# A feed-forward loop over token tiles: the fourth tile's gate and up move right behind the third's

## The chip, the core and the metric

The kernel runs on one core of a Trainium2 chip. The metric is device time of one execution in microseconds (us). Before the change it is 1071.04 us, the median of 3 runs (1065.42 to 1078.87). Five engines work side by side, each through its own list of instructions in order, and meet through semaphores: TensorE (PE: matmuls and transposes; its weight loads are listed as PEld), VectorE (DVE), ScalarE (ACT), GpSimd (POOL) and SyncE (SP), which issues the DMAs here.

## What is computed

Four blocks over 16 sequences of 256 tokens with 128 features, each followed by a residual sum and a layer norm: a selective-scan block, a feed-forward block with quantised operands, a differential attention, and a three-layer perceptron with +1/-1 weights. The change touches the second one:

```
def fp4_quant_dequant(x):               # blocks of 16 along the last dimension
    scale = max(max|x| over the block / 6, 1e-12)
    xn = x / scale
    return nearest value of the grid {0, .5, 1, 1.5, 2, 3, 4, 6} to |xn|, * sign(xn) * scale

gate = quant(x) @ quant(w_gate).T        # 128 -> 352
y    = quant(x) @ quant(w_up).T          # 128 -> 352
h    = silu(gate) * y
out  = quant(h) @ quant(w_down).T        # 352 -> 128
x    = layernorm(x + out)
```

## The kernel before

The 4096 tokens are 32 tiles of 128, in 8 groups of 4 tiles. `x_all` keeps all tokens on chip. The phases follow each other: the scan, the feed-forward part, the attention, the perceptron, and neighbouring phases are interleaved at their borders.

The feed-forward part is a software pipeline written out by hand. Each engine has its own function `step(n)`, a generator of 8 pieces, and the order of the calls in it is the order of that engine's instructions. In step n:

- TensorE does gate and up of the four tiles of group n (`gate_up(n, j)`: the gate matmul is L1151, the up matmul L1153, each listed as two instructions), and for group n-2 the transposes of the quantised hidden tile (`turn`, L1164), the residual through an identity (`residual`, L1171) and the down projection (`down`, L1179). At its end it transposes group n+1's quantised x (L1108).
- ScalarE does the SiLU of each gate tile (`silu`, L1040), copies transposed tiles out of PSUM (`took_h`, L1047 and L1049), takes the absolute value of the hidden group n-1 (L1075) and of the x group n+2 (L1090), and squares and normalises group n-3 (L1056, L1063).
- VectorE multiplies SiLU and up (`hidden(n, j)`, L876), quantises the hidden group n (`scale_h`: maximum L914, scale L916, reciprocal L918, correction L920, scaling L923), takes the hidden group n-1 further (`magic_h` L928, `back_h` L934), and does the same for x of group n+2 (`scale_x` L885 to L894, `magic_x` L899, `back_x` L905). `magic` multiplies by a large number whose addition and subtraction rounds to the grid.
- GpSimd adds and subtracts it: for the hidden group n-1 L992 and L997, over 1408 columns, and for x of group n+2 L1004 and L1008, over 512 columns. It also takes the inverse root for the norm of group n-3 (L983, L986).

The order around the change in a step of VectorE is: `hidden 0`, `magic_h`, `hidden 1`, `scale_x`, `hidden 2`, `magic_x`, `hidden 3`, `scale_h`, `back_h`, `back_x`. GpSimd's list is: norm of n-3, L992, L997, L1004, L1008.

`hidden(n, j)` waits for the up matmul and the SiLU of its tile. `magic_x` waits for ScalarE's Abs (L1090), which waits for `scale_x`. L992 waits for `magic_h`, L997 for L992 by a semaphore, L1004 for `magic_x`. `scale_h` waits for all four tiles of the group. The gate matmul of tile j waits for the SiLU two tiles before (two banks of PSUM, `gp`); from step 6 (`LONE`) on there is one bank, because the attention has taken the other, and it waits for the SiLU of the tile before. The up matmul of tile j waits for the product two tiles before.

Steps -1 to 1 run beside the end of the scan, steps 2 to 5 alone, steps 6 to 10 beside the first pieces of the attention; that is written in `parts`, by `side_by_side`, which alternates the pieces of two generators. The attention's first pieces project and rotate a sequence: TensorE's L1644 over `a_xT`, ScalarE's copy L1606, GpSimd's multiplications L1502.

Of the kernel before, what the change touches and what calls it, by code (L numbers as in the profile page):

```python
# [63 lines left out]
def wait(eng, sem, value):  # L64

    if not (isinstance(value, int) and value <= 0):
        eng.wait_ge(sem, value)
# [119 lines left out]
def ffn_blocks(k, m):  # L187
    return k.x_all[:, bass.ds(GT * m, GT), :].rearrange("p a (b e) -> p (a b) e", e=QB)
# [555 lines left out]
def ffn_phase(nc, k, scan):  # L744
# [75 lines left out]
    def gate_bank(n, j):  # L820

        return gp[j % 2 if n < f.LONE else 0]

    def has(m):
        return 0 <= m < GROUPS
# [43 lines left out]
    def vector(dve):  # L869
        def hidden(n, j):  # L870
            if has(n):
                dve.wait_ge(up_ready, GT * n + j + 1)
                dve.wait_ge(silu_ready, GT * n + j + 1)
                if j == 0:
                    wait(dve, h_step, 5 * n)
                nc.vector.tensor_tensor(hid[:, j], sg[:, j], up[j % 2][:, 0:HID], ALU.mult).then_inc(hid_ready, 1)  # L876

        def scale_x(m):
            b = 5 * (m - 1)
            src = ffn_blocks(k, m)  # L880
            dve.wait_ge(x_back, m)
            dve.wait_ge(scan.norm_chain, m + 1)
            if m == 1:
                dve.wait_ge(scan.hcd_ready, scan.on_dve(GROUPS, 0))
            nc.vector.tensor_reduce(x_scale, src, AX.X, ALU.max, apply_absolute_value=True).then_inc(x_step, 1)  # L885
            dve.wait_ge(x_step, b + 1)
            nc.vector.tensor_scalar(x_scale, x_scale, 1.0 / 6.0, 1e-12, ALU.mult, ALU.max).then_inc(x_step, 1)
            dve.wait_ge(x_step, b + 2)
            nc.vector.reciprocal(x_inv, x_scale).then_inc(x_step, 1)
            dve.wait_ge(x_step, b + 3)  # L890
            nc.vector.tensor_scalar(x_inv, x_inv, 1.0 - 2.0 ** -22, None, ALU.mult).then_inc(x_step, 1)
            dve.wait_ge(x_step, b + 4)
            wait(dve, x_add, m - 1)
            nc.vector.tensor_tensor(qx.xs, src, x_inv.unsqueeze(2).broadcast_to([P, NXB, QB]),  # L894
                                    ALU.mult).then_inc(x_step, 1)

        def magic_x(m):
            dve.wait_ge(x_abs, m)
            nc.vector.tensor_scalar(qx.magic[:], qx.magic[:], 1.0, 2.0 ** 22 + 2.0, ALU.max,  # L899
                                    ALU.mult).then_inc(x_magic, 1)  # L900

        def back_x(m):
            dve.wait_ge(x_sub, m)
            dve.wait_ge(x_turned, m)
            nc.vector.tensor_tensor(qx.out, qx.q, x_scale.unsqueeze(2).broadcast_to([P, NXB, QB]),  # L905
                                    ALU.mult).then_inc(x_back, 1)

        def scale_h(m):
            b = 5 * m
            src = hid[:].rearrange("p a (b e) -> p (a b) e", e=QB)  # L910
            scale = h_scale[m % 2]
            dve.wait_ge(hid_ready, GT * m + GT)
            wait(dve, h_back, m - 1)
            nc.vector.tensor_reduce(scale, src, AX.X, ALU.max, apply_absolute_value=True).then_inc(h_step, 1)  # L914
            dve.wait_ge(h_step, b + 1)
            nc.vector.tensor_scalar(scale, scale, 1.0 / 6.0, 1e-12, ALU.mult, ALU.max).then_inc(h_step, 1)  # L916
            dve.wait_ge(h_step, b + 2)
            nc.vector.reciprocal(h_inv, scale).then_inc(h_step, 1)  # L918
            dve.wait_ge(h_step, b + 3)
            nc.vector.tensor_scalar(h_inv, h_inv, 1.0 - 2.0 ** -22, None, ALU.mult).then_inc(h_step, 1)  # L920
            dve.wait_ge(h_step, b + 4)
            wait(dve, h_add, m)
            nc.vector.tensor_tensor(hxs[:], src, h_inv.unsqueeze(2).broadcast_to([P, NHB, QB]),  # L923
                                    ALU.mult).then_inc(h_step, 1)

        def magic_h(m):
            dve.wait_ge(h_abs, m + 1)
            nc.vector.tensor_scalar(hmagic[:], hmagic[:], 1.0, 2.0 ** 22 + 2.0, ALU.max,  # L928
                                    ALU.mult).then_inc(h_magic, 1)

        def back_h(m):
            dve.wait_ge(h_sub, m + 1)
            wait(dve, h_turned, GT * (m - 1))
            nc.vector.tensor_tensor(hout[:, m % 2], hq[:], h_scale[m % 2].unsqueeze(2).broadcast_to([P, NHB, QB]),  # L934
                                    ALU.mult).then_inc(h_back, 1)

        nc.vector.memset(eps[:], LN_EPS).then_inc(const_ready, 1)

        def step(n):
            hidden(n, 0)  # L940
            yield
            if n == 0:
                back_x(1)
            if has(n - 1):
                magic_h(n - 1)
            yield
            hidden(n, 1)
            if has(n + 2):
                scale_x(n + 2)
            yield  # L950
            hidden(n, 2)
            if has(n + 2):
                magic_x(n + 2)
            yield
            hidden(n, 3)
            yield
            if has(n):
                scale_h(n)
            yield
            if has(n - 1):  # L960
                back_h(n - 1)
            yield
            if has(n + 2) and n >= 0:
                back_x(n + 2)
            yield

        return step
# [67 lines left out]
    def scalar(act):  # L1035
        def silu(n, j):
            if has(n):
                act.wait_ge(gate_ready, GT * n + j + 1)
                wait(act, hid_ready, GT * (n - 1) + j + 1)
                nc.scalar.activation(sg[:, j], gate_bank(n, j)[:, 0:HID], ACT.Silu).then_inc(silu_ready, 1)  # L1040

        def took_h(m, j):
            if has(m):
                act.wait_ge(h_turned, GT * m + j + 1)
                wait(act, down_ready, GT * m + j - 1)
                src = th[j % 2][:, 0:len(HC) * P].rearrange("p (c t) -> p c t", c=len(HC))
                nc.scalar.activation(hqT[:, j % 2, 0:full], src[:, 0:full], ACT.Copy)  # L1047
                rows = HC[-1][1]
                nc.scalar.activation(hqT[0:rows, j % 2, full], src[0:rows, full], ACT.Copy).then_inc(h_copied, 1)  # L1049

        def squares(m):

            act.wait_ge(down_ready, GT * m + GT)
            wait(act, rstd_ready, m)
            for j in range(GT):
                last = nc.scalar.activation(square[:, j], dn[:, j], ACT.Square, scale=DM ** -0.5,  # L1056
                                            accum_out=var[:, j:j + 1])
            last.then_inc(var_ready, 1)

        def normalize(m):  # L1060
            act.wait_ge(rstd_ready, m + 1)
            for j in range(GT):
                last = nc.scalar.activation(k.x_all[:, GT * m + j, :], dn[:, j], ACT.Copy, scale=rstd[:, j:j + 1])  # L1063
            last.then_inc(norm_chain, 1)

        def step(n):
            silu(n, 0)
            if has(n - 3):
                squares(n - 3)
            yield  # L1070
            m = n - 1
            if has(m):
                act.wait_ge(h_step, 5 * m + 5)
                wait(act, h_sub, m)
                nc.scalar.activation(hmagic[:], hxs[:], ACT.Abs).then_inc(h_abs, 1)  # L1075
            silu(n, 1)
            yield
            took_h(n - 2, 0)
            took_h(n - 2, 1)
            yield  # L1080
            if has(n - 3):
                normalize(n - 3)
            silu(n, 2)
            yield
            m = n + 2
            if has(m):

                act.wait_ge(x_step, 5 * (m - 1) + 5)
                wait(act, x_sub, m - 1)
                nc.scalar.activation(qx.magic[:], qx.xs, ACT.Abs).then_inc(x_abs, 1)  # L1090
            took_h(n - 2, 2)
            yield
            silu(n, 3)
            yield
            took_h(n - 2, 3)
            yield
            if has(n + 1) and n >= 0:
                took_x(act, n + 1)
            yield

        return step
# [37 lines left out]
    def tensor(pe):  # L1139
# [43 lines left out]
        def step(n):  # L1183
# [5 lines left out]
            turn(n - 2, 1)  # L1189
            yield  # L1190
            gate_up(n, 2)
            residual(n - 2)
            down(n - 2, 0)
            yield
            turn(n - 2, 2)
            down(n - 2, 1)
            yield
            gate_up(n, 3)
            yield
            turn(n - 2, 3)  # L1200
            down(n - 2, 2)
# [1084 lines left out]
```

## Time and profile before

| | |
|---|---|
| median of 3 runs | 1071.04 us |
| lowest, highest | 1065.42, 1078.87 us |
| the profiled execution | 1068.53 us, span 1066.7 us, mean granted TensorE clock 0.964 of full speed |
| busy over the span | PE 912.0 us (85%), DVE 891.7 (84%), POOL 788.1 (74%), ACT 731.5 (69%) |
| the feed-forward steps 0 to 5 | about 484 to 560 us of the span |

The feed-forward steps lie between the scan, which ends at about 477 us, and the attention, whose first maxima start at 596 us. Over the whole span DVE and PE are about equally busy, and the chain of waits (the chain of work that ended last, followed back from the last instruction) is shared between them: DVE 28%, PE 26%, issue 17%, ACT 15%, DMA 7%, POOL 4%. So one has to read the stage itself, from the timeline of each engine, which lists instructions in order of time with the idle time before each and what ended it.

### The profile page before, as it was taken

Reading aid. Unit: us, or ns where it says so; the run is one execution under the profiler, and the core shown is the slowest. Engines: PE = TensorE matmul, PEld = TensorE weight load, DVE = VectorE, ACT = ScalarE, POOL = GpSimd, SP = SyncE. Lnnn points to the kernel's source line nnn. Section 1 sums busy time; section 2 is a strip of 40 time slices with the busy share of each in tenths; the row PEclk is TensorE's granted clock in tenths of the full one; section 3 lists DMA queues with packets and bytes.
Section 4 is the critical chain, followed back from the end, with each engine's and each line's share of the span. In section 5 each row is a group of like instructions: output and inputs, shape, how many; then the busy total and the mean of one; then the engine's idle time right before and its main releaser. Section 6 shows DMA issues by size and latency. Waiting matters only on the chain.

```text
span 1066.7 us, 14636 instructions
## 1 busy us (share of the span) xinstructions
PE 912.0 (85%) x4466; PEld 481.7 (45%) x4482; DVE 891.7 (84%) x1337; ACT 731.5 (69%) x1600; POOL 788.1 (74%) x560
## 2 busy tenths in 40 slices
PE   7697979897989797786888679999999898699995
PEld 3233434342434343233556454565655543355453
DVE  4799999999999999998885667787777783479996
ACT  3776868686868686544565457777777768777872
POOL 2798998989898989875777734575756535767773
PEclk9899999899999999899999889999999999899998
DMA  4762535353434434003400323332323210000001
GB/s 149 318 239 79 205 113 200 118 199 119 177 142 152 166 141 177 0 1 81 66 0 16 104 76 90 92 99 83 99 83 102 80 47 2 0 2 12 18 21 30
DMA packets 35168, 104.03 MB, mean 98 GB/s; under 512 B 3659, under 2 KB 22475, under 8 KB 24395
## 3 DMA queue, kind: packets, MB, share of 16 engines
q1 hardware_dynamic: 35095, 103.16, 28.9%
q8 instruction: 34, 0.56, 0.2%
q14 instruction: 39, 0.32, 0.1%
HBM read 93.84 MB, written 8.91 MB: 96 GB/s over the span
## 4 chain that ended last, share of the span: by engine, by line
DVE 28%; PE 26%; issue 17%; ACT 15%; DMA 7%; POOL 4%; SPq 4%; DVEq 1%; POOLq 0%; ACTq 0%
PE bank L1644 11%; DVE bank L333 8%; PE bank L610 8%; DMA ks<-parts 6%; PE bank L2002 4%; DVE m_hC L342 4%; DVE a_nm L1410 3%; ACT bank L461 2%; DVE m_hS L333 2%; ACT L461 2%; SPq L1362 1%; DVE m_du L347 1%; SPq L1373 1%; DVE x_all L122 1%; DVE bank L914 1%
## 5 line engine op out<-in xcount | busy, mean ns | idle before, releaser
L610 PE MATMUL bank<-m_hC,ident 128*128 128x512 f32 x512 | 257.8, 627 | 61.4 <-POOL m_hC L568 22.7
L558 POOL TENSOR_TENSOR m_dBu<-m_du,m_Bt 128x1024 f32<-128x1024 f32 x128 | 299.3, 2356 | 12.6 <-DMA m_Bt<-bcd 11.8
L333 DVE TENSOR_TENSOR_SCAN bank<-bank,m_dBu 128x512 f32<-128x512 f32 x184 | 222.4, 1219 | 16.5 <-ACT bank L461 12.6
L1410 DVE TENSOR_REDUCE a_nm<-bank 128x2 f32<-128x512 f32 x256 | 169.3, 687 | 66.7 <-PE bank L1644 66.5
L1581 ACT ACTIVATE late<-bank 128x512 f32<-128x512 f32 x256 | 148.9, 600 | 65.2 <-PE bank L1644 63.4
L610 PEld LDWEIGHTS bank<-m_hC,ident 128*128 128x128 f32 x512 | 93.9, 196 | 203.9 <-issue 111.5
L461 ACT ACTIVATE bank<-m_delta,early 128x510 f32<-128x510 f32 x256 | 170.0, 677 | 0.3
L1644 PE MATMUL bank<-ks,qs 72*128 72x256 bf16 x512 | 100.4, 279 | 28.7 <-DMA ks<-parts 16.8
L342 DVE TENSOR_TENSOR m_hC<-bank,m_Ct 128x512 f32<-128x512 f32 x184 | 123.3, 670 | 0.0
L568 POOL TENSOR_TENSOR m_hC<-m_hS,m_Ct 128x512 f32<-128x512 f32 x72 | 94.6, 1315 | 26.6 <-DVE m_hS L333 26.6
L458 ACT ACTIVATE bank<-m_zero 128x2 f32<-128x2 f32 x181 | 31.2, 173 | 115.5 <-DVE m_hC L342 114.9
L1644 PE MATMUL bank<-qs,ks 99*128 99x256 bf16 x512 | 99.8, 277 | 4.5 <-ACT late L1581 3.1
L333 DVE TENSOR_TENSOR_SCAN m_hS<-bank,m_dBu 128x512 f32<-128x512 f32 x72 | 86.8, 1206 | 0.0
L2002 PE MATMUL bank<-qs,early 128*128 128x512 bf16 x374 | 85.7, 382 | 0.5
L1644 PEld LDWEIGHTS bank<-qs,ks 99*128 99x128 bf16 x512 | 43.3, 99 | 60.8 <-ACT late L1581 52.3
L1644 PEld LDWEIGHTS bank<-ks,qs 72*128 72x128 bf16 x512 | 44.6, 99 | 52.5 <-DVE a_nm L1410 25.3
L1644 PE MATMUL bank<-late,vx 128*32 128x512 f32 x512 | 68.0, 604 | 0.0
L1952 POOL TENSOR_TENSOR ks<-ks 128x512 f32<-128x512 f32 x32 | 38.5, 1204 | 32.7 <-ACT ks L1977 24.4
L610 PE MATMUL bank<-m_xT,m_wk 128*128 128x512 f32 x128 | 61.2, 624 | 0.0
L2002 PEld LDWEIGHTS bank<-qs,early 128*128 128x128 bf16 x384 | 37.3, 99 | 44.9 <-issue 2.8
L1518 POOL TENSOR_TENSOR a_part<-a_res,a_part 128x512 bf16<-128x512 f32 x16 | 18.5, 1155 | 47.4 <-ACT a_part L1600 47.4
L1525 POOL TENSOR_TENSOR a_rms<-a_ms_eps,neg_half 128x16 f32<-128x16 f32 x16 | 47.0, 2940 | 1.3
(217 smaller groups left out, 1797.1 us busy)
## 6 DMA issues: line engine op xcount, KB each, us to landing
m_Bt<-bcd SPq DMA_DIRECT2D x32, 1024.0 KB, 6.3
m_Ct<-bcd SPq DMA_DIRECT2D x32, 1024.0 KB, 6.6
qs<-parts SPq DMA_DIRECT2D x16, 576.0 KB
ks<-parts SPq DMA_DIRECT2D x48, 192.0 KB
parts<-a_part SPq DMA_DIRECT2D x32, 192.0 KB, 2.2
out<-x_all SPq DMA_DIRECT2D x8, 256.0 KB, 2.3
vx<-in_vrow SPq DMA_DIRECT2D x4, 256.0 KB
qs<-in_fill SPq DMA_DIRECT2D x1, 768.0 KB
```

Source lines behind the costliest of these rows:

```text
L333: nc.vector.tensor_tensor_scan(out, decay, dBu[:, g % RD], 0.0, ALU.mult, ALU.add).then_inc(scan_ready, 1)
L342: nc.vector.tensor_tensor(hC[:, g % RH], dA[g % RA][:].rearrange("p a b -> p (a b)"), Ct[:, s], ALU.mult).then_inc(hcd_ready, 1)
L461: nc.scalar.activation(dA[g % RA][:, :, 1:SEQ], delta[:, n % 2, c].rearrange("p (a b) -> p a b", a=2)[:, :, 1:SEQ], ACT.Exp, scale=decay[: ...
L558: nc.gpsimd.tensor_tensor(dBu[:, g % RD:g % RD + CH], du[:, n % 2], Bt[:, s].unsqueeze(1).broadcast_to([P, CH, GTOK]), ALU.mult).then_inc( ...
L568: nc.gpsimd.tensor_tensor(hC[:, g % RH], hS[:, on_pool(n, i) % RS], Ct[:, s], ALU.mult).then_inc(hcp_ready, 1)
L610: return nc.tensor.matmul(out, lhsT, rhs, start=start, stop=stop)
L1410: nc.vector.tensor_reduce(nm[:, slot % 2, q, 2 * pair:2 * pair + 2], s1[i % 2][:], AX.X, ALU.max, negate=True).then_inc(max_ready, 1)
L1525: nc.gpsimd.tensor_tensor(rms[:], ms_eps[:], k.neg_half[:, 0:TS * NH], ALU.pow).then_inc(rms_chain, 1)
L1581: nc.scalar.activation(pT[:, u // 2, u % 2], s2[u % 2][:], ACT.Exp, scale=float(HD) ** -0.25).then_inc(exp_ready, 1)
L1644: return nc.tensor.matmul(out, lhsT, rhs, start=start, stop=stop)
L1952: nc.gpsimd.tensor_tensor(rest_tile(s, c), full_tile(s, c), part_tile(s, q, c, 0), ALU.subtract).then_inc(s.rest_ready, 1)
L2002: return nc.tensor.matmul(out, lhsT, rhs, start=start, stop=stop)
```

## The change

In all three engines' `step(n)` the call for the fourth tile moves up to stand right behind the third tile's. On TensorE that is ahead of `residual`, `down 0`, `turn 2` and `down 1`; on ScalarE ahead of the Abs of x and `took_h 2`; on VectorE ahead of `magic_x`. Nothing is added or removed, and GpSimd's and SyncE's lists are the same.

```diff
@@ vector, step(n)
             hidden(n, 2)
+            hidden(n, 3)
             if has(n + 2):
                 magic_x(n + 2)
             yield
-            hidden(n, 3)
             yield
@@ scalar, step(n)
             silu(n, 2)
+            silu(n, 3)
             yield
             m = n + 2
             if has(m):
...
             took_h(n - 2, 2)
             yield
-            silu(n, 3)
             yield
@@ tensor, step(n)
             gate_up(n, 2)
+            gate_up(n, 3)
             residual(n - 2)
             down(n - 2, 0)
             yield
             turn(n - 2, 2)
             down(n - 2, 1)
             yield
-            gate_up(n, 3)
             yield
```

VectorE's list in a step from 2 to 5, around `magic_x`. L894 is the last instruction of `scale_x`, L876 the products of SiLU and up, L899 `magic_x`, L914 the first of `scale_h`.

```order
 L891 TENSOR_SCALAR bank<-bank 128x32
 L894 TENSOR_TENSOR early<-x_all,bank 128x512
-L876 TENSOR_TENSOR late<-late,bank 128x352
+L876 TENSOR_TENSOR late<-late,bank 128x352 x2
 L899 TENSOR_SCALAR early<-early 128x512
-L876 TENSOR_TENSOR late<-late,bank 128x352
 L914 TENSOR_REDUCE bank<-late 128x88
 L916 TENSOR_SCALAR bank<-bank 128x88
```

The product of the fourth tile now stands ahead of `magic_x` (L899), which stands directly before `scale_h`.

TensorE's list in the same steps, from the third tile's gate and up (L1151, L1153) on; L1171 is the residual, L1179 a down projection.

```order
 L1151 MATMUL bank<-early,late 128x352
 L1153 MATMUL bank<-early,late 128x352
+L1151 MATMUL bank<-early,late 128x352
+L1153 MATMUL bank<-early,late 128x352
 L1171 MATMUL bank<-x_all,ident 128x512
 L1179 MATMUL bank<-early,late 128x128 x3
```

The fourth tile's pair now stands ahead of the residual; before, it stood behind the second down projection.

## Rows read from the trace of the kernel before

**Rows 1.** Chain of waits, 470 to 690 us: start, duration, engine, tile and line.

```profile
526.71 0.53 DVE late L876
...
564.13 3.17 POOL late L992
```

**Rows 2.** Timeline, DVE, step 3: start, duration, engine, line, operation, shapes, [idle before].

```profile
520.52 0.51 DVE L876 TENSOR_TENSOR late<-late,bank 128x352 f32<-128x352 f32 x1
520.95 0.89 DVE L928 TENSOR_SCALAR late<-late 128x1408 f32<-128x1408 f32 x1
...
524.38 0.51 DVE L876 TENSOR_TENSOR late<-late,bank 128x352 f32<-128x352 f32 x1
525.16 0.43 DVE L899 TENSOR_SCALAR early<-early 128x512 f32<-128x512 f32 x1 [0.27 <-ACT early L1090]
526.71 0.52 DVE L876 TENSOR_TENSOR late<-late,bank 128x352 f32<-128x352 f32 x1 [1.12 <-PE bank L1153]
527.26 1.63 DVE L914 TENSOR_REDUCE bank<-late 128x88 f32<-128x1408 f32 x1
...
534.36 0.89 DVE L928 TENSOR_SCALAR late<-late 128x1408 f32<-128x1408 f32 x1
```

**Rows 3.** Timeline, DVE, steps 0 to 2: h2, then L928 and L914.

```profile
486.89 0.51 DVE L876 TENSOR_TENSOR late<-late,bank 128x352 f32<-128x352 f32 x1
...
488.65 1.63 DVE L914 TENSOR_REDUCE bank<-late 128x88 f32<-128x1408 f32 x1
...
494.71 0.90 DVE L928 TENSOR_SCALAR late<-late 128x1408 f32<-128x1408 f32 x1 [0.41 <-ACT late L1075]
...
499.90 1.63 DVE L914 TENSOR_REDUCE bank<-late 128x88 f32<-128x1408 f32 x1
...
507.00 0.89 DVE L928 TENSOR_SCALAR late<-late 128x1408 f32<-128x1408 f32 x1
...
513.86 1.63 DVE L914 TENSOR_REDUCE bank<-late 128x88 f32<-128x1408 f32 x1
```

**Rows 4.** Timeline, POOL, steps 3, 6 and 7.

```profile
521.92 3.17 POOL L992 TENSOR_TENSOR late<-late 128x1408 f32<-128x1408 f32 x1 [2.70 <-DVE late L928]
525.17 3.46 POOL L997 TENSOR_TENSOR late<-late 128x1408 f32<-128x1408 f32 x1
...
567.38 3.16 POOL L997 TENSOR_TENSOR late<-late 128x1408 f32<-128x1408 f32 x1
...
587.77 1.26 POOL L1502 TENSOR_TENSOR a_rc<-a_qk,aprm 128x512 f32<-128x512 f32 x1
```

**Rows 5.** Timeline, DVE, at two places outside the stage.

```profile
434.35 2.30 DVE L163 TENSOR_SCALAR early<-early 128x512 int32<-128x512 int32 x1
...
742.70 1.17 DVE L1428 CAST a_nmp<-a_nmr 128x32 bf16<-128x32 f32 x1
```

**Rows 6.** Timeline, POOL, at the same two places.

```profile
434.02 2.35 POOL L558 TENSOR_TENSOR m_dBu<-m_du,m_Bt 128x1024 f32<-128x1024 f32 x1
...
742.67 1.15 POOL L1518 TENSOR_TENSOR a_part<-a_res,a_part 128x512 bf16<-128x512 f32 x1 [2.65 <-ACT a_part L1600]
```

**Rows 7.** Timeline, PE, steps 2, 3 and 7.

```profile
506.10 1.54 PE L1164 MATMUL bank<-ident,late 128*128 128x128 f32 x6 [3.68 <-DVE late L934]
...
521.37 0.75 PE L1153 MATMUL bank<-early,late 128*128 128x352 f32 x2
...
581.35 1.12 PE L1171 MATMUL bank<-x_all,ident 128*128 128x512 f32 x2 [0.26 <-ACT x_all L1063]
```

**Rows 8.** Timeline, ACT, step 7: SiLU of the third tile, copy for the rotation.

```profile
581.17 0.48 ACT L1040 ACTIVATE late<-bank 128x352 f32<-128x352 f32 x1
...
585.91 0.60 ACT L1606 ACTIVATE a_qk<-bank 128x512 f32<-128x512 f32 x1 [0.83 <-PE bank L1644]
```

**Rows 9.** Windows: stretch, us, busy (x instructions) by engine, PE clock, DMA share, GB/s.

```profile
506.00:509.50 3.50, 3.40 (x11) 2.62 (x12) 3.43 (x8) 1.83 (x6) 1.54 (x1) 0.57 1.04 135
520.00:533.40 13.40, 10.78 (x58) 7.65 (x58) 11.71 (x20) 8.23 (x28) 10.35 (x6) 1.00 0.01 4
```

## The prediction

> **Names.** Step n of the feed-forward part has tile products h0 to h3 of group n on VectorE (L876), gate and up matmuls g0 to g3 on TensorE (L1151, L1153), SiLUs on ScalarE (L1040). Around them on VectorE: magic_h (L928, for group n-1), scale_x (L885 to L894) and magic_x (L899, both for group n+2), scale_h (from L914, group n) and the two scalings back (L934, L905). On GpSimd an add (L992) and a subtract (L997) finish group n-1. In the code magic_h stands in step n; I count the scale_h that follows it as the same step's. All times are us.
>
> **What bounds the kernel now.** I read the chain of waits first, over 470 to 690, to see who sets the pace there. Through steps 1 to 5 it runs mostly on VectorE, and h3 of each step is in it, followed at once by scale_h; it then passes to GpSimd's L992 of group 5, and from there to GpSimd, a transfer and the attention part [rows 1]. So what VectorE gains or loses before L992 of group 5 starts at 564.13 shifts all that follows. Then I read the timeline of VectorE in one step [rows 2]: from magic_h at 520.95 everything is back to back up to h2 at 524.38; it idles 0.27 before magic_x, because magic_x waits for ScalarE's Abs, and 1.12 before h3, because g3 stands on TensorE behind the residual and two down projections. scale_h starts 6.31 after magic_h. Steps 4 and 5 repeat this to a hundredth. The step lasts 534.36 - 520.95 = 13.41. Last I read GpSimd's timeline beside it [rows 4]: L992 starts 0.97 after magic_h, and L997 at 525.17, which is 0.01 after magic_x.
>
> **Taking the idle time away, alone.** With g3 behind g2, up of the third tile is issued at 521.37, so g3 and its up follow in two pieces of 0.59 to 0.60 and are out of TensorE by about 523.3 [rows 7]. h2 to h3 then is VectorE's own spacing, 0.43 (520.95 - 520.52 [rows 2]). magic_x would follow at 524.38 + 0.43 + 0.43 = 525.24. It started at 525.16 when Abs released it, so Abs is over by then and nothing that the program names holds it at 525.24. scale_h would start 0.42 later, at 4.71 after magic_h instead of 6.31: 1.60 saved a step.
>
> **What magic_x runs into.** It now comes 525.24 - 525.17 = 0.07 *after* L997 instead of 0.01 before it, and that order matters. Both read and write SBUF. Where such a VectorE instruction started 0.03 after a GpSimd one, it took 1.17 instead of some 0.18 and ended 0.05 after GpSimd's; where a 2.35 long GpSimd multiply had begun 0.33 earlier, a tensor_scalar of 512 columns took 2.30 and ended 0.28 after it [rows 5, 6]. Conversely L997 takes 3.46 where magic_x came first and 3.16 where there is none [rows 4]: there GpSimd waited. Who starts first has it to itself, to a few hundredths. The shift of 0.07 does not come from a wait that might go away: L997 hangs on magic_h by 0.97 + 3.17 + 0.08, and magic_x on the same magic_h by VectorE's fixed spacings. Anything that delays VectorE in between only puts magic_x deeper into L997. So the collision comes in every step from 1 to 5; step 0 has no L997.
>
> **Sum.** L997, now not held, ends at 525.17 + 3.16 = 528.33. magic_x ends 0.28 later, as the row of 2.30 does (the same size), at 528.61, and scale_h starts at 528.62, which is 7.67 after magic_h.
> Step 3: 528.62 - 527.26 = +1.36, and the same in 4 and 5: +4.08.
> Step 1: 494.71 + 7.67 = 502.38 against 499.90: +2.48 (here h3 was not late before, so there is only the loss).
> Step 2: 507.00 + 7.67 = 514.67 against 513.86: +0.81 (h3 waited longer here before).
> Step 0: 486.89 + 0.86 + 0.42 = 488.17 against 488.65: -0.48 [rows 3].
> Together +6.9. From scale_h to the next magic_h VectorE's order is unchanged, and GpSimd's two later operations for x begin when magic_x is done and have L914 to L934, over 6, as cover.
> The unknown is how long a 3.16 instruction holds VectorE, since no row shows a wait longer than about 1.9 (2.30 less the 0.43 that magic_x itself takes). If the hold were capped there, scale_h would start at 525.24 + 1.87 + 0.42 = 527.53: +0.27 for steps 3 to 5, +1.39, -0.28 and -0.48 for the others, together +1.4. If nothing held, see the first rival. I take the full hold, since both rows end with GpSimd's instruction, a short one and a long one, not after a fixed time.
> The Trainium skill, "SBUF — State Buffer", section "SBUF: two separate sides", goes further than these rows: the pair of ports is an exclusive lock, kept for the whole instruction by whichever starts first. By that rule the sum is the +6.9, by the cap it would be +1.4.
>
> **The moves that cost nothing.** On TensorE the residual of steps 2 to 5 comes some 0.5 later and the last down projection 0.7 earlier, inside an idle time of about 2 before the next turns. ScalarE's third-to-fourth SiLU (under 0.5) lies before the Abs, which waits for VectorE's scale_x anyway (the 0.27 of rows 2 is the end of that detour). In steps 6 and 7 the gate bank is single, so g3 waits for the SiLU of g2, and the residual and the attention's projections with it. Step 7: that SiLU ends at 581.65, then g3 and up take 1.3, so the residual goes from 581.35 to 583.0. ScalarE's copy for the rotation, 585.91 to 586.51 now, would end at 588.16, and GpSimd wants it at 587.77: 0.4 late [rows 4, 7, 8]. In step 6 the same delay is 1.2 and hidden. The chain passes this place through the transfer of the tile before [rows 1], so I put it at 0 and keep 0.4 for the range. That h3 of steps 6 and 7 comes over 4 earlier is worth nothing for the same reason.
> On VectorE, GpSimd and SP nothing is added; no DMA moves.
>
> Base: the profiled execution took 1068.53, 2.5 under the median of the three runs, 1071.04. 1068.53 + 6.9 = 1075.4. The three runs lie 13 apart; a lead of 0.01 for magic_x is thin, and some executions of the kernel before may lose it in some steps, which the changed one can do no longer. That is why I do not add the 2.5, but leave room for it above.
>
> **Rivals.**
> 1. *magic_x is not held* (it wins, or the two share). Steps 1 to 5 have scale_h 4.71 after magic_h: -0.48, -2.15 and three times -1.60, with step 0 -0.48: together -7.9, 1060.6. For it: h3's idle time really goes. Against it: rows 5 and 6. Chance 0.14.
> 2. *The hold is partial or comes in some steps only*, between the two: +1.4 by the cap, 1066 to 1073. Chance 0.08.
> 3. *TensorE's clock.* The longer step leaves TensorE idle for about 2.0 + 1.36 + 0.7 = 4.1 before the turns. In step 2, after 3.68 of idle time, its granted clock was 0.57 over the next 3.5, near the lower of its two levels, 1.2 GHz, and six transposes took 1.54; in step 3 it was 1.00, the upper one [rows 7, 9]. Work of a step is 10.78 at full clock. The new step of 14.8 has 4.0 to spare, and 3.5 of low clock cost at most 1.75 of it: hidden, though I expect to see it. It decides once more than 4.0 of full-speed work is done at half speed. If a whole step stayed low, 21.6 against 14.8 would add 6.8 in each of steps 2 to 5, 27 in all: 1103. Against it: the clock came back within step 2. Chance 0.03.
> 4. *The 0.4 of step 7 and its like do reach the chain* on top of the forecast, moving also which attention casts meet GpSimd: 1076 to 1079. Chance 0.07.
> My forecast has 0.68.
>
> **Numbers.** 1075.4. The first rival at 1060.6 holds 0.14 and the third 0.03; leaving the lower part of the one and the whole of the other out, and giving the forecast the scatter of the runs shown (about 6 either way, more upward for the 2.5), the range is 1063 to 1083. A change of 2%, about what a measurement of this kernel can tell from none, would be 1049.6 or 1092.5: only the third rival gets there. Faster 0.02, same 0.95, slower 0.03.
>
> **What would show it.** In the profile after: h2 and h3 0.43 apart in steps 0 to 5; L899 with about 3.4 instead of 0.43 in five of its seven rows, L997 with 3.16 instead of 3.45; scale_h 7.7 after magic_h; steps of 14.8; L992 of group 5 near 571.0. Wrong, if L899 stays at 0.43 (rival 1: L992 near 556), if L899 is near 2.3 (rival 2), or if h3 waits for TensorE (rival 3).

## The result, and the profile after

| | before | changed |
|---|---|---|
| median of 17 runs each (lowest to highest) | 1072.71 us (1065.42 to 1078.87) | 1080.96 us (1073.25 to 1088.04) |
| ratio, 95% interval | 1 | 1.0079 (1.0053 to 1.0105) |
| the profiled execution | 1068.53, span 1066.7, clock 0.964 | 1084.06, span 1082.3, clock 0.948 |

The change makes the kernel 8.3 us slower (5.7 to 11.3 by the interval). The ratios here and below leave out the few runs that lie more than 1.5% above the fastest of their kernel (one of B, 1209.61, and two of the kernel before). Times below are us; steps, h3, magic_x and so on are named as in the prediction. "Stage" is the time from the first scale_x (L885) to L992 of group 5, the place from which the chain passes on.

VectorE's timeline of step 3 in the changed kernel, the counterpart of [rows 2] (start, duration, engine, line, operation, shapes, count, [idle before and its releaser]):

```profile
522.49 0.88 DVE L928 TENSOR_SCALAR late<-late 128x1408 f32<-128x1408 f32 x1
...
525.91 0.94 DVE L876 TENSOR_TENSOR late<-late,bank 128x352 f32<-128x352 f32 x2
526.77 3.38 DVE L899 TENSOR_SCALAR early<-early 128x512 f32<-128x512 f32 x1
530.08 1.61 DVE L914 TENSOR_REDUCE bank<-late 128x88 f32<-128x1408 f32 x1
```

h2 and h3 now stand in one row (x2, 0.94), with no idle time around them. But L899, 0.43 before, takes 3.38, and scale_h starts 530.08 - 522.49 = 7.59 after magic_h. No row shows VectorE idle: the wait is inside the instruction's duration. What it waits for stands on GpSimd, to be read against [rows 4]:

```profile
523.45 3.17 POOL L992 TENSOR_TENSOR late<-late 128x1408 f32<-128x1408 f32 x1 [2.65 <-DVE late L928]
526.71 3.17 POOL L997 TENSOR_TENSOR late<-late 128x1408 f32<-128x1408 f32 x1
530.24 1.28 POOL L1004 TENSOR_TENSOR early<-early 128x512 f32<-128x512 f32 x1 [0.36 <-DVE early L899]
...
569.47 3.17 POOL L992 TENSOR_TENSOR late<-late 128x1408 f32<-128x1408 f32 x1 [5.32 <-DVE late L928]
...
593.46 1.27 POOL L1502 TENSOR_TENSOR a_rc<-a_qk,aprm 128x512 f32<-128x512 f32 x1 [0.28 <-ACT a_qk L1606]
```

L997 starts at 526.71, 0.06 ahead of L899, and ends at 529.88; L899 ends at 530.15, 0.27 later. L997 itself is down from 3.46 to 3.17. The stage is 569.47 - 476.12 = 93.35 against 87.01, +6.3. The chain of waits (start, duration, engine, tile, line) now goes through the held instruction:

```profile
497.53 3.29 DVE early L899
...
526.77 3.38 DVE early L899
...
556.26 3.38 DVE early L899
...
569.47 3.17 POOL late L992
```

TensorE's clock, by windows as in [rows 9] (stretch, us, busy of PE, PEld, DVE, ACT, POOL, PE clock, DMA share, GB/s), is at its lower level of 1.2 GHz in steps 2 and 4 and at the upper one, 2.4, in step 3:

```profile
506.00:509.50 3.50, 2.57 (x9) 2.05 (x10) 3.50 (x6) 2.19 (x6) 0.71 (x1) 0.50 0.99 136
520.00:533.40 13.40, 10.51 (x58) 7.77 (x58) 13.12 (x19) 8.25 (x27) 10.16 (x7) 1.00 0.01 2
536.00:542.00 6.00, 5.72 (x14) 3.96 (x15) 4.97 (x11) 3.54 (x13) 3.79 (x2) 0.50 0.00 0
```

Each low stretch stands behind idle time of TensorE: 4.84 in step 2 (3.68 before [rows 7]) and 4.15 in step 4, where the six transposes then take 1.54. The length of the idle time alone does not settle it: a second profile of the kernel before had six transposes at 1.54 in step 4 behind 2.04. The low clock makes h3 of step 4 late. It costs nothing there, because magic_x is held to the end of L997 wherever it comes inside it: it starts later and is held shorter (2.00), and scale_h still comes 7.59 after magic_h (537.16, not shown, to 544.75).

```profile
536.27 1.54 PE L1164 MATMUL bank<-ident,late 128*128 128x128 f32 x6 [4.15 <-DVE late L934]
```

```profile
542.39 0.52 DVE L876 TENSOR_TENSOR late<-late,bank 128x352 f32<-128x352 f32 x1 [1.28 <-PE bank L1153]
542.83 2.00 DVE L899 TENSOR_SCALAR early<-early 128x512 f32<-128x512 f32 x1
544.75 1.61 DVE L914 TENSOR_REDUCE bank<-late 128x88 f32<-128x1408 f32 x1
```

### The profile page after: what moved, and what is told of

It is laid out like the page before. It is cut to its first block, busy times and chain, and to the rows that moved or that the text cites. A ratio compares the mean times of both kernels' runs of the same rounds, so it can differ in the third digit from the quotient of the medians.

```text
span 1082.3 us, 14652 instructions
## 1 busy us (share of the span) xinstructions
PE 926.3 (86%) x4482; PEld 489.6 (45%) x4482; DVE 904.2 (84%) x1337; ACT 732.2 (68%) x1600; POOL 787.2 (73%) x560
## 4 chain that ended last, share of the span: by engine, by line
DVE 28%; PE 25%; issue 17%; ACT 14%; DMA 7%; POOL 4%; SPq 4%; DVEq 1%; POOLq 0%; ACTq 0%
PE bank L1644 11%; DVE bank L333 8%; PE bank L610 7%; DMA ks<-parts 6%; PE bank L2002 4%; DVE m_hC L342 4%; ACT bank L461 2%; DVE a_nm L1410 2%; DVE m_hS L333 2%; ACT L461 2%; SPq L1362 2%; DVE early L899 1%; SPq L1373 1%; DVE m_du L347 1%; DVE x_all L122 1%
## 5 line engine op out<-in xcount | busy, mean ns | idle before, releaser
L2002 PE MATMUL bank<-qs,early 128*128 128x512 bf16 x384 | 88.2, 384 | 0.0
L1502 POOL TENSOR_TENSOR a_rc<-a_qk,aprm 128x512 f32<-128x512 f32 x16 | 20.3, 1272 | 39.5 <-DVE late L1447 28.4
```

Source lines behind the costliest of these rows:

```text
L2002: return nc.tensor.matmul(out, lhsT, rhs, start=start, stop=stop)
```

## The experiments

The theory: VectorE's new order lets GpSimd's L997 start first, and a magic_x that starts behind it is held to its end; that is the whole loss. Rivals: the two engines share something and slow each other whatever the order; TensorE and ScalarE lose by their own new order; the low clock costs.

Ratios below are to the kernel before on the same chip, with 95% intervals.

| kernel | median, before beside it | ratio (95%) | stage | scale_h after magic_h, steps 1 to 5 |
|---|---|---|---|---|
| before | | | 87.01, 90.16 | 5.19, 6.86 or 8.3, then 6.31 or 7.16 |
| changed | | 1.0079 | 93.35, 93.36 | 7.59 |
| A: changed, subtract waits for magic_x | 1067.09, 1073.59 | 0.9939 (0.9913 to 0.9965) | 79.23 | 4.63 (one 4.84) |
| B: VectorE's move alone | 1082.68, 1073.59 | 1.0080 (1.0053 to 1.0108) | 94.28 | 7.59 (one 7.73) |
| C: TensorE's and ScalarE's moves alone | 1073.73, 1073.59 | 1.0004 (0.9979 to 1.0029) | 84.45 | 5.10, 8.13, 5.09, 5.10, 5.09 |
| D: subtract in two halves | 1071.05, 1073.59 | 0.9996 (0.9967 to 1.0025) | 85.88 | 6.10 |
| E: magic_x in another form | 1067.18, 1072.96 | 0.9933 (0.9902 to 0.9963) | 80.38 | 4.88 to 4.90 |
| F: before, subtract waits | 1073.75, 1072.96 | 1.0007 (0.9977 to 1.0037) | 90.16 | 5.18, 8.33, 7.16, 7.15, 6.31 |
| G: A with the old place in steps 6 and 7 | 1064.59, 1072.96 | 0.9931 (0.9902 to 0.9960) | 78.56 | 4.62 to 4.65 |
| H: before, moved in steps 6 and 7 only | 1075.10, 1074.98 | 0.9992 (0.9958 to 1.0025) | 90.19 | 5.19, 8.33, 7.16, 7.15, 6.32 |

A ratio is not made from the two medians beside it and can differ from their quotient by 0.002 (D). Stages without a median were read from a kernel's profiles alone; before and changed were each profiled twice.

### A. The subtract waits for magic_x

```diff
                 pool.wait_ge(h_add, m + 1)
+                if has(n + 2):
+                    pool.wait_ge(x_magic, n + 2)
                 nc.gpsimd.tensor_tensor(hq[:], hq[:], hmagic[:], ALU.subtract).then_inc(h_sub, 1)
```

> The changed kernel, but GpSimd's subtract L997 also waits for magic_x, so that VectorE always has the shared access first. Theory (first start holds it for the whole instruction): L899 takes 0.43 in all steps, L997 3.45, scale_h starts about 4.7 after magic_h, and the stage is 7.9 us shorter than before, 14 shorter than with the change alone: about 0.993 of the kernel before. Rival (VectorE's magic_x is slow for another reason, such as a late Abs from ScalarE or TensorE's lower clock): L899 or the wait before it stays long and the time stays at 1.008.

VectorE and GpSimd in one step of this kernel (its L999 is the old L997):

```profile
517.12 0.89 DVE L928 TENSOR_SCALAR late<-late 128x1408 f32<-128x1408 f32 x1 [0.36 <-ACT late L1077]
...
521.41 0.42 DVE L899 TENSOR_SCALAR early<-early 128x512 f32<-128x512 f32 x1
521.75 1.62 DVE L914 TENSOR_REDUCE bank<-late 128x88 f32<-128x1408 f32 x1
```

```profile
518.09 3.17 POOL L992 TENSOR_TENSOR late<-late 128x1408 f32<-128x1408 f32 x1 [0.83 <-DVE late L928]
521.98 3.17 POOL L999 TENSOR_TENSOR late<-late 128x1408 f32<-128x1408 f32 x1 [0.71 <-DVE early L899]
```

With the order of the two starts turned round, magic_x takes 0.42 and GpSimd pays 0.71 of waiting, which nobody on VectorE sees. (The subtract was expected at 3.45; it takes 3.17, because the added wait starts it after magic_x has ended.) The stage falls from 93.35 to 79.23, 7.8 under the profile of before. One added wait turns 0.8% slower into 0.6% faster; the difference of the two ratios, 0.0140, is 15 us, and the stage holds 14.1 of it. So the loss is the order of these two starts. The rival of mutual slowing falls: L999 takes 3.17 with VectorE's L914 and what follows it beside it, and L997 took 3.16 where there was no magic_x [rows 4].

### B. VectorE's move alone

```diff
             hidden(n, 2)
+            hidden(n, 3)
             if has(n + 2):
                 magic_x(n + 2)
             yield
-            hidden(n, 3)
             yield
```

> Only VectorE's order is changed; TensorE and ScalarE keep the old one, so h3 is ready only where it was before. Theory: magic_x, now behind h3, always meets L997 and is held to its end whatever h3 does; scale_h 7.6 after magic_h as with the whole change, so the same +6 to +7 us (1.006). Rival (the cost comes from moving TensorE's or ScalarE's work): within 1 or 2 us of before, since h3 then only changes places with a short instruction.

VectorE's half of the change alone, made on the kernel before, gives the whole loss: 1.0080 against the change's 1.0079. The hold appears in four of the five steps and fills up to the same end. (In step 2 h3 comes so late that magic_x starts at 516.83, just behind L997's end at 516.80, and takes 0.42; scale_h is 7.73 after magic_h by h3 alone.) In the step shown h3 comes late, from TensorE's old order, and L899 takes the 1.48 that is left of L997:

```profile
530.00 0.52 DVE L876 TENSOR_TENSOR late<-late,bank 128x352 f32<-128x352 f32 x1 [1.82 <-PE bank L1153]
530.44 1.48 DVE L899 TENSOR_SCALAR early<-early 128x512 f32<-128x512 f32 x1
531.84 1.61 DVE L914 TENSOR_REDUCE bank<-late 128x88 f32<-128x1408 f32 x1
```

```profile
528.46 3.17 POOL L997 TENSOR_TENSOR late<-late 128x1408 f32<-128x1408 f32 x1
```

### C. TensorE's and ScalarE's moves alone

```diff
             hidden(n, 2)
-            hidden(n, 3)
             if has(n + 2):
                 magic_x(n + 2)
             yield
+            hidden(n, 3)
             yield
```

(made on the changed kernel, so that only VectorE has its old order)

> Only TensorE's and ScalarE's orders are changed; VectorE keeps magic_x ahead of h3. Theory: magic_x keeps its 0.01 lead over L997 wherever Abs is on time, and h3 stands ready behind it: scale_h 5.2 after magic_h instead of 6.3 in steps 3 to 5 (-1.1 each). In step 2, where TensorE's clock is low, the fourth SiLU comes late and stands ahead of Abs, so magic_x may be late and held (+0.7). In all -3 to -5 us (0.996). Rival (the lead of 0.01 is luck): held in several steps, up to +6.

The total is that of before (1.0004), and the 0.996 that was expected lies outside the interval (0.9979 to 1.0029). The stage did get shorter, 84.45 against 87.01 and 90.16; why the total does not show it is open, but L992 of group 5 to that of group 7 takes 33.43 in this profile against 32.3 before, which takes 1.1 back. In four of five steps scale_h comes 5.09 to 5.10 after magic_h, so g3's earlier place does remove most of h3's wait. In step 2 the clock was low, the third and fourth SiLU came late (the last at 509.88), and with them the Abs behind them; magic_x then starts behind L997 and is held:

```profile
510.90 3.39 DVE L899 TENSOR_SCALAR early<-early 128x512 f32<-128x512 f32 x1 [0.35 <-ACT early L1091]
514.21 0.51 DVE L876 TENSOR_TENSOR late<-late,bank 128x352 f32<-128x352 f32 x1
```

```profile
510.83 3.17 POOL L997 TENSOR_TENSOR late<-late 128x1408 f32<-128x1408 f32 x1
```

A lateness of 0.08 on ScalarE (0.35 of idle time instead of 0.27) costs 2.96 on VectorE. The order is decided anew in each step, by whatever is late.

### D. The subtract in two halves

```diff
-                nc.gpsimd.tensor_tensor(hq[:], hq[:], hmagic[:], ALU.subtract).then_inc(h_sub, 1)
+                half = NHB // 2
+                nc.gpsimd.tensor_tensor(hq[:, 0:half], hq[:, 0:half], hmagic[:, 0:half], ALU.subtract)
+                nc.gpsimd.tensor_tensor(hq[:, half:], hq[:, half:], hmagic[:, half:], ALU.subtract).then_inc(h_sub, 1)
```

> The changed kernel with L997 as two instructions of half the columns (about 1.6 each). Theory (the hold lasts as long as the GpSimd instruction that has begun): magic_x waits only for the first half, L899 about 1.8, scale_h 6.0 after magic_h: about -1.2 us to before (0.999). Rival (GpSimd keeps it for its run of work, or the hold is a fixed time): L899 stays at 3.4 and the time at 1.006 to 1.008.

```profile
525.04 1.89 DVE L899 TENSOR_SCALAR early<-early 128x512 f32<-128x512 f32 x1
526.85 1.62 DVE L914 TENSOR_REDUCE bank<-late 128x88 f32<-128x1408 f32 x1
```

```profile
524.96 1.68 POOL L998 TENSOR_TENSOR late<-late 128x704 f32<-128x704 f32 x1
526.60 1.86 POOL L999 TENSOR_TENSOR late<-late 128x704 f32<-128x704 f32 x1
```

The hold ends with the instruction that was running, not with the work that GpSimd has queued: magic_x gets in behind the first half, and now the second half is the longer one (1.86). Its 1.89 against 3.38, with the instruction ahead of it 1.68 against 3.17, is the same 1.49 twice.

### E. magic_x in a form that takes its factor from PSUM

The factor now comes from 32 columns of a PSUM bank that hold the constant.

```diff
+                nc.vector.memset(factor, 2.0 ** 22 + 2.0).then_inc(factor_ready, 1)
...
-            nc.vector.tensor_scalar(qx.magic[:], qx.magic[:], 1.0, 2.0 ** 22 + 2.0, ALU.max,
-                                    ALU.mult).then_inc(x_magic, 1)
+            nc.vector.scalar_tensor_tensor(out=qx.magic[:], in0=qx.magic[:], scalar=1.0,
+                                           in1=factor.unsqueeze(2).broadcast_to([P, NXB, QB]),
+                                           op0=ALU.max, op1=ALU.mult).then_inc(x_magic, 1)
```

> The changed kernel, but magic_x takes its factor from a constant in PSUM (one SBUF input, no doubled rate, about 0.69 instead of 0.43 for 512 columns), and meets L997 as before. Theory (only the doubled-rate form shares an access with GpSimd): it is not held although it starts after L997; L899's counterpart takes 0.69, L997 3.16, scale_h about 4.9 after magic_h, 6 to 6.5 us under the kernel before in the stage (0.994). Rival (any VectorE work on SBUF that starts after a GpSimd instruction is held): 3.4 as in the changed kernel, 1.008.

```profile
523.62 0.68 DVE L904 SCALAR_TENSOR_TENSOR early<-early,bank 128x512 f32<-128x512 f32 x1
524.22 1.62 DVE L920 TENSOR_REDUCE bank<-late 128x88 f32<-128x1408 f32 x1
```

```profile
523.55 3.18 POOL L1003 TENSOR_TENSOR late<-late 128x1408 f32<-128x1408 f32 x1
```

Here GpSimd again starts first, by 0.07, and magic_x is not held at all: 0.68, slower by itself than 0.43, but 2.70 shorter than when held. All seven of them take 0.68. The products are not held either: in the changed kernel h2 and h3 (L876, one operand in PSUM) run from 525.91 inside L992 (523.45 to 526.62) and take 0.94 for the two. So it is not any VectorE work beside L997 that is held, but this form: a TENSOR_SCALAR from SBUF to SBUF. Which of the two differences counts, the operation's form or its second operand in PSUM, this run does not separate.

The Trainium skill, "SBUF — State Buffer", section "SBUF: two separate sides", says that VectorE and GpSimd lock a pair of ports, for the whole instruction, and that on VectorE's side this touches instructions in the modes that use both ports, or, against a GpSimd instruction that reads SBUF, with two inputs in SBUF. A, D and E agree: 0.42 when VectorE is first, 1.89 behind 1.68, 3.38 behind 3.17, and 0.68 without a hold for the other form.

### F. The same wait on the kernel before

The edit is A's, made on the kernel before.

> The kernel before, with GpSimd's L997 waiting for magic_x, so that the lead of 0.01 can never be lost. If executions of the kernel before do lose it now and then, and that makes part of their 13 us of scatter, this is 1 to 3 us faster in the median and scatters less. If they never lose it, 1.000, since in the profile L997 is held by magic_x anyway.

No difference (1.0007; the interval from 0.9977 rules out a gain of 3 us, not one of 1 or 2). The profiles of the kernel before and of H say why: there magic_x starts first in each of steps 1 to 5, and L899 takes 0.43 at most. F itself cannot show that, since its subtract waits for magic_x. What this run taught is something else. Its stage is 90.16, not 87.01, and the steps differ from [rows 2]:

```profile
526.42 0.43 DVE L899 TENSOR_SCALAR early<-early 128x512 f32<-128x512 f32 x1 [0.27 <-ACT early L1092]
528.83 0.52 DVE L876 TENSOR_TENSOR late<-late,bank 128x352 f32<-128x352 f32 x1 [1.98 <-PE bank L1155]
529.38 1.63 DVE L914 TENSOR_REDUCE bank<-late 128x88 f32<-128x1408 f32 x1
```

```profile
522.00:526.00 4.00, 4.00 (x11) 2.20 (x10) 3.86 (x9) 2.50 (x10) 2.82 (x1) 0.57 0.00 0
```

h3 waits 1.98 for TensorE instead of 1.12, behind four microseconds at a clock of 0.57 in a step that had 1.00 in the first profile. It is not the added wait that does this: the second profile of before, below, has a stage of 90.16 as well. The stage of the old order depends on the clock; that of the changed kernel was 93.35 and 93.36 in its two profiles.

### G and H. Steps 6 and 7

G is A, with SiLU and gate and up of the fourth tile in their old place for steps 6 and 7, where the gate bank is single; H is the kernel before with them in the new place for these steps alone. The edit of G for the SiLU (that for gate and up has the same form, and H is its opposite; LONE is 6):

```diff
             silu(n, 2)
-            silu(n, 3)
+            if n < f.LONE:
+                silu(n, 3)
...
+            if n >= f.LONE:
+                silu(n, 3)
...
```

> The kernel in which the subtract waits (the fast one), with the fourth tile's place on TensorE and ScalarE undone for steps 6 and 7 alone. Theory (there g3 waits for the SiLU of g2 on the one gate bank and delays the attention's projection, 0.4 us on GpSimd's rotation): L992 of group 5 to that of group 7 is 32.3 instead of 32.7; in the time at most 1 us better (0.993 of the kernel before). Rival (most of what the changed kernel lost behind the stage, some 2 us, came from there): 2 us or more better.

> The kernel before, with the fourth tile moved up on TensorE and ScalarE in steps 6 and 7 alone (VectorE's order there is the same in both). Theory: from L992 of group 5 to that of group 7 it takes 32.7 instead of 32.3, nothing else changes: 1.000 to 1.001 of the kernel before. Rival (the part of the loss that lies behind the stage comes from here): 1.002 or more.

By the totals neither is told apart: G against A is 0.9931 against 0.9939, H 0.9992. In the traces, L992 of group 5 to L992 of group 7 takes 32.34 in G and 32.67 in A, and 33.83 in H against 32.30 to 32.32 in the profiles of before. H was expected at 32.7. Over all twelve profiles this stretch takes 32.30 to 32.35 in the five with the old place on TensorE and ScalarE (before twice, B, F, G) and 32.67 to 34.64 in the seven with the new one (the changed kernel twice, A, C, D, E, H). So the move costs these steps 0.3 to 2.3, too little to show in the totals. G has the lowest median of all; the traces speak for it, the interval does not decide.

### The two kernels once more

A second profile of each, on one chip, to see which parts of the difference repeat.

> The changed kernel once more, for a second trace. From the first scale_x to L992 of group 5: 93.3 again, since every step ends with the held magic_x, 7.59 behind magic_h, whatever TensorE's clock does. From L992 of group 7 to the end: 470 to 480 like the others, longer the more of it has the low clock. If it is above 480 again, the change also costs something there.

> The kernel before once more. From the first scale_x to L992 of group 5: 87 to 91, since h3 waits for TensorE, and so for its clock, in steps 2 to 5. From L992 of group 7 to the end: 470 to 480. If magic_x lost its lead of 0.01 in some step, L899 shows 3.4 there.

The changed kernel took 1080.82, the one before 1072.64. The stage, and the stretch from L992 of group 7 to the end, as windows. Changed, second profile:

```profile
475.66:569.02 93.36, 70.45 (x320) 47.34 (x321) 87.64 (x127) 48.09 (x144) 56.59 (x38) 0.91 0.22 43
603.59:1079.00 475.41, 421.72 (x3006) 247.82 (x3020) 354.91 (x688) 333.19 (x714) 281.91 (x267) 0.96 0.20 56
```

Before, second profile:

```profile
475.41:565.57 90.16, 70.68 (x320) 47.24 (x321) 75.46 (x127) 48.25 (x144) 57.83 (x39) 0.92 0.23 44
597.89:1070.80 472.91, 419.58 (x3006) 246.94 (x3022) 354.74 (x688) 332.53 (x714) 281.73 (x267) 0.96 0.19 56
```

And the same windows of the first pair, before:

```profile
477.12:564.13 87.01, 66.39 (x321) 44.52 (x322) 75.46 (x127) 47.90 (x144) 57.83 (x39) 0.98 0.24 46
596.45:1066.70 470.25, 416.82 (x3006) 245.70 (x3022) 355.13 (x688) 332.91 (x714) 281.69 (x267) 0.97 0.20 57
```

Changed:

```profile
602.15:1082.30 480.15, 426.75 (x3021) 250.42 (x3019) 356.25 (x688) 333.32 (x714) 282.00 (x267) 0.94 0.19 55
```

VectorE's busy time of the stage (the third number in a row after the stretch's length) is 75.46 in both profiles of before, 86.74 and 87.64 in the changed one: the hold is counted as work. By place:

| changed less before | first pair | second pair |
|---|---|---|
| up to the first scale_x | -1.0 | +0.25 |
| stage | +6.3 | +3.2 |
| L992 of group 5 to L992 of group 7 | +0.4 | +2.25 |
| the rest | +9.9 | +2.5 |
| span | +15.6 | +8.2 |

The third line of the second pair is the detour of steps 6 and 7, which is not hidden once the clock is low; the chain of waits of the changed kernel's second profile goes through it (TensorE's residual, the copy L1606, the rotation L1502). TensorE in step 6 of the changed kernel's second profile, and then GpSimd's rotation, late by 1.87:

```profile
570.71 1.38 PE L1153 MATMUL bank<-early,late 128*128 128x352 f32 x2
571.88 1.64 PE L1171 MATMUL bank<-x_all,ident 128*128 128x512 f32 x2
```

```profile
577.63 1.28 POOL L1502 TENSOR_TENSOR a_rc<-a_qk,aprm 128x512 f32<-128x512 f32 x1 [1.87 <-ACT a_qk L1606]
```

In the first profile of the changed kernel the same two rows of TensorE are 0.76 and 1.02, and the rotation of step 6 is not late at all.

## Why the prediction was right, point by point

**The total.** 1075.4 was forecast, 1080.96 came, inside the range, with the sign and the verdict of no 2% difference. The gain of moving h3 and g3 exists (A) and is more than undone by what magic_x runs into (B).

**The idle time taken away.** 4.71 after magic_h was worked out for a step without a hold; A shows 4.63 in four steps of five. The 0.08 is the last term: scale_h starts 0.34 after magic_x does (521.75 - 521.41), not 0.42, since a start can lie before the recorded end of the instruction ahead. Without the hold the stage would be 7.9 shorter by the forecast; A measured 7.8 against the first profile, and 10.9 against the other three with the old order, for the reason given below under the sum.

**The hold.** 7.67 was forecast, 7.59 measured, in all five steps and in both profiles; the difference is the same 0.08. The choice of the full hold over the cap of 1.87 was the term that decided the sign, and it was right. The full hold was argued from a row of 2.30 and one of 1.17, and D shows directly that the length is that of the other instruction.

**Which starts first.** The forecast was 0.07 behind L997; it is 0.06 to 0.08 where h3 is on time, and more where h3 is late. That magic_x cannot win in the new order was right, and in C it loses even in the old one.

**The sum of the stage.** +6.9 forecast, +6.3 measured in the profile pair on which it was built; most of the difference is the 0.08 above, once in each of six steps. This is the part that came out well partly by luck. The steps of 6.31 were taken as the kernel's own, but they need TensorE at its full clock: three other profiles with the old order (F, H, and before again) have 8.3 in step 2 and 7.15 to 7.16 in steps 3 and 4, and a stage of 90.16 to 90.19. Against these the stage loses only 3.2. The prediction saw that step 2 of [rows 3] was longer and that its clock was 0.57 [rows 9], and did not draw the consequence that another execution may have that in steps 3 and 4 too.

**The clock as rival 3.** Its mechanism was seen as described (0.50 in steps 2 and 4, back to 1.00 between) and is hidden inside the stage, as forecast. It never held a whole one of steps 2 to 5. But two of the signs listed were drawn too narrowly: h3 does wait for TensorE in step 2 (0.60) and step 4 (1.28), which was to mean rival 3, and L899 takes 2.69 and 2.00 there instead of 3.4. That wait only takes the place of a part of the hold.

**Steps 6 and 7.** Costed at 0, with 0.4 kept for the range. This term was mis-sized: in the first profile the 0.4 of step 7 does go through to L992 of group 7 (32.68 against 32.32), and the 1.2 of step 6 "and hidden" is hidden only at full clock; it was 1.9 late in the second profile and 1.1 in H's. Over all twelve profiles the stretch is 0.3 to 2.3 longer with the new place. Whether that reaches the end of the program no run shows: H's interval, 0.9958 to 1.0025, has room for its 1.5 as well as for no loss at all.

**Where the 5.6 above the forecast lies.** 4.2 of it is the base: the profiled execution of 1068.53 was 4.2 under the median of 17 runs, 1072.71. The other 1.4 is the difference of the medians, 8.3, against the 6.9 of the sum. The base was left at 1068.53 with the argument that other executions of the kernel before may lose the lead of 0.01. None of the three profiles that could show it (two of before, and H) does. What the old order loses in H, in F and in the second profile of before is the full clock in steps 3 and 4, and this the new order does not get back: its stage is 3.2 longer than those too. The argument should have been made from the clock in [rows 9], and then for a base of about the median.

**What stays open.** From L992 of group 7 on, all kernels run the same order of work, and yet this stretch took from 470.3 to 480.1 over twelve profiles. It goes roughly with TensorE's clock: by windows of 2 us the shortest had 30 us of it at the low level and the longest 54, and half speed for 24 more us would be 12 if TensorE set the pace throughout (an estimate); 9.9 were seen. The clock is not all: B had 46 us at the low level and took 480.0. Kernels of the old order cover 470.3, 472.9, 478.4 (H) and 479.8 (F), the changed one 475.4 and 480.1. So two profiles cannot say whether the change makes that part slower. Over the runs the mean granted clock of the changed kernel is 0.950, that of before 0.953 to 0.955 (beside the experiments); in the stage alone it is 0.89 and 0.91 against 0.98 and 0.92. The medians' 8.3 are so accounted for within their interval by either stage difference, 6.3 or 3.2, with 0.4 to 2.25 for steps 6 and 7 and a rest of 1.6 to 2.8, which a lower clock behind the stage could make up; that it comes from there is not shown.

## What to carry to other kernels

When independent instructions are reordered on VectorE, look at what GpSimd starts within a few tenths of a microsecond of each: a move that closes an idle gap can turn a race that was won by 0.01 or less into one that is lost for the length of the other engine's longest instruction. Such a loss does not show as idle time but as one instruction with two durations (0.42 and 3.38 of the same shape). Three remedies worked: a wait that makes GpSimd, which has time to spare, come second (0.994 of the kernel before), another form of the short instruction (0.993), and, for half of it, shorter instructions on GpSimd (1.000).

## What the runs showed of the hardware that was not expected

- The margin is fine and yet steady. A start 0.06 behind costs 2.96 (3.38 less 0.42), and a hold came in five steps out of five, in both profiles. A lead of 0.01 (in some steps the two starts are the same to the hundredth, as 498.93 in step 1 of before) was never lost in steps 1 to 5 of the three profiles that have VectorE's and ScalarE's old order there and no added wait.
- The held TENSOR_SCALAR of 512 columns (L899) ends 0.27 to 0.29 after GpSimd's instruction in each case (530.15 against 529.88; 526.93 against 526.64 in D), less than the 0.43 that it takes by itself. Part of what makes up its 0.43 can thus lie under the hold.
- TensorE's low clock in a feed-forward step of the old order differs between executions: steps 3 and 4 had it in three profiles of four. A single profile's durations behind a TensorE wait carry that with them (6.31 or 7.16 for the same step).
